# Eleven more edge-convolution steps projected in the largest-scores stage; early skip and mix fills moved into six written-out rounds of the scores pass

## The reference, cut to what matters

```python
e  = einsum('ehd,ehd->eh', q[src], k[dst]) * scale     # scores pass
m  = segment_max(e, dst)                               # largest-scores stage
ex = exp(e - m[dst])                                   # attention pass, with its sums per node
agg = segment_sum(ex / denom[dst] * v[src], dst)
skip = feat @ Wskip.T + bskip                          # "skip" fills; out*gate @ Wproj are the "mix" fills
msg = (edge_attr @ W_edge.T + b_edge) * h[src]         # edge convolution, 384 -> 256 per edge
agg = segment_sum(msg, dst)
fx = proj(expmap0(ft + b_res))                         # ball attention's last norm, taken up in the top stage
```

## Time and profile before

| what | value |
|---|---|
| median of 3 runs | 2938.04 us (2937.12 to 2939.76) |
| the profiled execution's own time | 2938.99 us |
| span of the profile (first to last instruction) | 2937.3 us |
| TensorE (PE) busy | 2614.2 us, 89% |
| VectorE (DVE) busy | 2130.9 us, 73% |
| ScalarE (ACT) busy | 1402.0 us, 48% |
| GpSimd (POOL) busy | 1069.7 us, 36% |

### The profile page before, as it was taken

The page is one execution under the profiler, slowest core; times in us unless marked ns, Lnnn a source line. Parts: engine busy times, 40 slices in busy tenths (PEclk is TensorE's granted clock), DMA queues, the critical chain, the costliest instruction groups (busy, mean ns, idle before and its releaser), DMA issues. The chain is left out here.

```text
span 2937.3 us, 54945 instructions
## 1 busy us (share of the span) xinstructions
PE 2614.2 (89%) x11923; PEld 2052.7 (70%) x11926; DVE 2130.9 (73%) x4283; ACT 1402.0 (48%) x2975; POOL 1069.7 (36%) x1184
## 2 busy tenths in 40 slices
PE   8777788779998999999989999999789978779698
PEld 6555555465556777777768888999678866657587
DVE  6687777868889665765348888888899969955321
ACT  3324323129884343443434444444489958755122
POOL 1677777722111000000016777666300018800043
PEclk9999999989999999999999999999889989989799
DMA  4799999937776100000036777667401130043343
GB/s 160 253 314 309 313 314 310 317 73 229 230 227 222 65 1 10 10 1 10 9 112 216 231 223 230 215 214 214 134 27 41 41 135 3 1 183 108 107 159 128
DMA packets 238294, 447.78 MB, mean 152 GB/s; under 512 B 29441, under 2 KB 127809, under 8 KB 236764
## 3 DMA queue, kind: packets, MB, share of 16 engines
q1 hardware_dynamic: 181214, 265.82, 27.7%
q0 software_dynamic: 56960, 180.47, 20.0%
HBM read 353.30 MB, written 93.87 MB: 152 GB/s over the span
## 5 line engine op out<-in xcount | busy, mean ns | idle before, releaser
L2065 PE MATMUL bank<-sums 128*128 128x256 f32 x2208 | 508.7, 381 | 2.0 <-PEq L117 1.6
L2164 POOL DMA_INDIRECT conv_h<-table_h,conv_ix x392 | 389.4, 993 | 241.0 <-ACT conv_ix L2125 152.8
L2065 PEld LDWEIGHTS bank<-sums 128*128 128x128 f32 x2208 | 408.6, 191 | 50.3 <-issue 2.0
L1840 ACT ACTIVATE area<-bank,nodes_bi,nodes_sc 128x320 f32<-128x320 f32 x320 | 197.4, 617 | 333.6 <-PE bank L1697 333.6
L731 POOL DMA_INDIRECT x<-table_qv,scores_ix x300 | 283.9, 946 | 162.2 <-ACT scores_ix L627 84.0
L2034 DVE SCALAR_TENSOR_TENSOR x<-bank,nodes_w,x 128x256 f32<-128x256 f32 x200 | 96.4, 483 | 215.7 <-PE bank L1708 215.6
L1454 PE MATMUL bank<-attend_pv,x 128*128 128x260 f32 x800 | 220.1, 404 | 26.7 <-POOL attend_pv L1384 24.6
L751 PE MATMUL bank<-sums,area 128*128 x800 | 224.2, 407 | 11.1 <-issue 5.9
L1454 PEld LDWEIGHTS bank<-attend_pv,x 128*128 128x128 f32 x800 | 137.5, 191 | 109.0 <-issue 62.5
L2125 ACT ACTIVATE conv_ix<-src 128x2 int32 x196 | 39.9, 203 | 336.1 <-DVE conv_msg L2188 329.3
L2204 DVE TENSOR_TENSOR sums<-sums,bank 64x256 f32 x392 | 163.8, 418 | 48.2 <-issue 36.3
(11 more groups left out here) (504 smaller groups left out, 5858.3 us busy)
## 6 DMA issues: line engine op xcount, KB each, us to landing
sums<-in_edges SPq DMA_DIRECT2D x184, 384.0 KB, 4.0
x<-edge_v SPq DMA_DIRECT2D x200, 256.0 KB, 3.0
edge_v<-x SPq DMA_DIRECT2D x150, 256.0 KB, 4.7
hidden_rows<-top_wide SPq DMA_DIRECT2D x25, 512.0 KB, 3.2
top_wd<-in_top_wd SPq DMA_DIRECT2D x8, 1024.0 KB, 13.7
projected<-spline_hst SPq DMA_DIRECT2D x8, 960.0 KB, 4.5
ball_hT<-projected SPq DMA_DIRECT2D x4, 1920.0 KB, 17.5
x<-in_x SPq DMA_DIRECT2D x10, 640.0 KB, 8.9
```

Of the source, the lines that this page charges most:

```text
L1840: nc.scalar.activation((h1, h2)[layer][:, o, hf * CW:(hf + 1) * CW], banks[n % HIDS][:, 0:CW], ACT.Relu, scale=sc[:, layer, e, o:o + 1], b ...
L2065: mm = nc.tensor.matmul(banks[u][:, g * F:(g + 1) * F], m.conv_eT[:, u, g, c], m.conv_w[:, c], start=False, stop=c == EC - 1, skip_group_c ...
L2164: nc.gpsimd.indirect_dma_start(out=h[:, u, g, :], out_offset=None, in_=m.d_h, in_offset=bass.IndirectOffsetOnAxis(ap=ix[:, u * G + g:u * G ...
```

## The change

- `AHEAD_STEPS` becomes 23 = `AHEAD_FIRST` 11 + `AHEAD_LAST` 12. The 12 stay in `node_layers`; the 11 are projected in `largest_scores`, 6 before the first scan's transposes and 5 before the second's, with edges loaded and results stored by SP. The loop in `edge_convolution` that takes one step of eight from `edges_ahead` then runs 23 passes.
- Of the early fills, 17 move into six written-out rounds (`FILLED` = 6) of the scores pass behind `MIXED`, two in the first and three in each of the others; 6 stay in the last round, 5 in the largest-scores stage.
- `FEWEST` becomes 2 * 23 + 3 = 49 for rounds of `UN` and `MIXED` + 6 + 2 = 30 for rounds of `RING` (26 and 24 before).
- SP loads the weights and bias for the 11 steps, 384 KB and 128 KB, in the scores pass.
- The start of the attention pass works in halves, with the clearing shared between ScalarE and GpSimd.
- At the end of the ball attention the first five tiles' roots, scaling and lengths are done, so that `lengths(0)` and `add(0)` leave the top stage.

```diff
+AHEAD_FIRST, AHEAD_LAST = 11, 12
+AHEAD_STEPS = AHEAD_FIRST + AHEAD_LAST
+FILLED = 6
+FEWEST = {UN: 2 * AHEAD_STEPS + 3, RING: MIXED + FILLED + 2}
-AHEAD_STEPS = 12
-FEWEST = {UN: 2 * AHEAD_STEPS + 2, RING: MIXED + 2}
...
-EARLY_IN_SCORES = 6
-EARLY_BESIDE_SCANS = (9, 8, 5)
+FILLS_AT = [{5: 0, 7: 1}] + [{1: 3 * k + 2, 4: 3 * k + 3, 7: 3 * k + 4} for k in range(FILLED - 1)]
+FILLS_IN_ROUNDS = sum(len(at) for at in FILLS_AT)
+EARLY_IN_SCORES = FILLS_IN_ROUNDS + 6
+EARLY_BESIDE_SCANS = (0, 0, len(EARLY_TILES) - EARLY_IN_SCORES)
+AHEAD_BESIDE_SCANS = (6, 5, 0)
...
@@ scores pass: SP, ScalarE, TensorE
                 sp.dma_start(m.wproj, a["mix_wproj"]).then_inc(early_loaded, 16)
+                sp.dma_start(m.ahead_w, a["gnn1_wedge"]).then_inc(ahead_loaded, 16)
+                sp.dma_start(m.ahead_b, a["gnn1_bedge"]).then_inc(ahead_loaded, 16)
+                sp.dma_start(m.first[:, 0:2 * UN * AHEAD_FIRST], m.d_steps[:, 0:2 * UN * AHEAD_FIRST]).then_inc(ahead_loaded, 16)
...
-                with act.Fori(MIXED + 1, rounds_of(act, m, RING)) as r:
+                for n, fills_at in enumerate(FILLS_AT):
+                    for u in range(RING):
+                        sources(MIXED + 1 + n, u)
+                        if u in fills_at:
+                            keep_early(fills_at[u])
+                with act.Fori(MIXED + 1 + FILLED, rounds_of(act, m, RING)) as r:
...
-                with pe.Fori(MIXED, last) as r:
+                for n, fills_at in enumerate(FILLS_AT):
+                    words = words_here()
+                    for u in range(RING):
+                        step(MIXED + n, u, words)
+                        if u in fills_at:
+                            early(fills_at[u])
+                    carry(words)
+                with pe.Fori(MIXED + FILLED, last) as r:
...
@@ largest-scores stage: SP, TensorE, ScalarE
+                for j in range(AHEAD_FIRST):
+                    edges_ahead(j)
+                    if j >= IN:
+                        store_ahead(j - IN)
...
+                def ahead(part):
+                    for j in steps_ahead(part):
+                        pe.wait_ge(ahead_in[j % IN], 16 * (j // IN + 1))
+                        pe.wait_ge(ahead_seeded, j + 1)
+                        for g in range(G):
+                            for k in range(EC):
+                                mm = nc.tensor.matmul(ahead_bank(j)[:, g * F:(g + 1) * F], ahead_eT[:, j % IN, g, k], m.ahead_w[:, k], start=False,
+                                                      stop=k == EC - 1, skip_group_check=True)
+                        mm.then_inc(ahead_made, 1)
...
-                early(0)
+                ahead(0)
...
-                    early(j + 1)
+                    ahead(j + 1)
+                pe.wait_ge(ahead_kept, AHEAD_FIRST)
+                early(2)
...
@@ attention pass: SP, start
-                sp.dma_start(m.first, m.d_steps[:, 0:2 * UN * AHEAD_STEPS]).then_inc(vec_loaded, 16)
+                sp.dma_start(m.first[:, 0:2 * UN * AHEAD_LAST], m.d_steps[:, 2 * UN * AHEAD_FIRST:2 * UN * AHEAD_STEPS]).then_inc(vec_loaded, 16)
+                sp.dma_start(m.first[:, 2 * UN * AHEAD_LAST:], m.d_steps[:, 0:UN]).then_inc(vec_loaded, 16)
...
@@ ball attention: ScalarE, VectorE
+                    if t == NT - 1:
+                        first_lengths(0, 2)
                     act.wait_ge(o_turned, t + 1)
...
+                first_add(0, 1)
                 keep(NT - 2)
+                first_add(1, U)
                 keep(NT - 1)
...
@@ top stage
-                lengths(0)
+                act.sem_inc(far_sq, U)
+                act.sem_inc(far, 1)
                 bend(0)
...
-                add(0)
-                add(1)
                 floor(0)
+                dve.sem_inc(added, U)
...
                 result(0)
                 normal(0)
+                add(1)
```

More of the change, by code:

```diff
@@ L119, in _ @@
         def _(sp):
[L120 to L124, removed]
+            clear_semaphores(nc, sp)
 def mean_and_variance(nc, c, stats, mv, work):
@@ L910, in _ @@
                         spread_out(last, u + UN - 1, words[-1])
[L911 to L917, removed]
+                    here = EARLY_IN_SCORES - FILLS_IN_ROUNDS
+                    for fill in range(u * here // RING, (u + 1) * here // RING):
+                        early(FILLS_IN_ROUNDS + fill)
             @block.vector
@@ L1103, in largest_scores, with steps_ahead, ahead_bank @@
         early_made, early_kept = st.sem("early_made"), st.sem("early_kept")
+        ahead_opened, ahead_seeded, ahead_made, ahead_kept = (
+            st.sem(x) for x in ("ahead_opened", "ahead_seeded", "ahead_made", "ahead_kept"))
+        IN, BANKS = 3, 3
+        ahead_eT = st.sb("ahead_eT", [P, IN, G, EC, P])
+        ahead_in = [st.sem(f"ahead_in{u}") for u in range(IN)]
+        ahead_stored = [st.sem(f"ahead_stored{u}") for u in range(2)]
+        def steps_ahead(part):
+            first = sum(AHEAD_BESIDE_SCANS[:part])
+            return range(first, first + AHEAD_BESIDE_SCANS[part])
+        def ahead_bank(j):
+            return banks[5 + j % BANKS][:, 0:G * F]
         def fills(part):
@@ L1367, in _ @@
                 distance(word, 0, 1)
+                for k, part in enumerate(halves):
+                    act.wait_ge(diff, 4 + k)
+                    nc.scalar.activation(m.probs[:, part], m.probs[:, part], ACT.Exp, scale=float(HD) ** -0.5).then_inc(exps, 1)
                 with act.Fori(0, last) as r:
@@ L1596, in _ @@
                     sp.dma_start(to, a[x]).then_inc(loaded, 16)
-                for j in range(IN_RING, AHEAD_STEPS):
+                for j in range(IN_RING, AHEAD_LAST):
                     edges_ahead(j)
@@ L1628, in _ @@
                         for u in range(OUT_RING + 2):
-                            sp.wait_ge(ahead_stored[u], 16 * sum(ahead_slot(j) == u for j in range(AHEAD_STEPS)))
+                            sp.wait_ge(ahead_stored[u], 16 * sum(ahead_slot(j) == u for j in range(AHEAD_LAST)))
                         sp.wait_ge(outs, TU * XQ * U)
@@ L1736, in _ @@
                 pe.wait_ge(ahead_w_in, 16)
-                for j in range(AHEAD_STEPS - 1):
+                for j in range(AHEAD_LAST - 1):
                     project_ahead(j)
@@ L2594, in output, with first_lengths @@
                     nc.scalar.activation(oT[:, t % 2], banks[6][:, 0:OC], ACT.Copy).then_inc(o_copied, 1)
+                def first_lengths(begin, end):
+                    for t in range(begin, end):
+                        act.wait_ge(first_added, t + 1)
+                        if t:
+                            act.wait_ge(first_squared, t)
+                        nc.scalar.activation(junk[:, 0:F], m.rows[:, t], ACT.Square, accum_out=far[:, t:t + 1]).then_inc(first_squared, 1)
                 for t in range(2):
```

161 lines of the change are left out of this document (120 added, 41 removed).

## The result

The changed kernel takes 3129.86 us (median of 4 runs, 3126.88 to 3131.05) where the kernel before takes 2937.58: ratio 1.0646, 95% interval 1.0633 to 1.0658, +192 us. The forecast was 3126 in a range of 3062 to 3150, and slower. The profiled execution takes 3131.05 us, with a span of 3129.1, 191.8 longer than before's.

A forecast was written before the change was run, and what follows sets the result against it. GpSimd's pace bounds the scores pass now, with DMA engines close behind; TensorE bounds attention and convolution. Terms 157.6 + 46.7 + 2 + 5 + 0.5 - 20.8 - 3 = +188.0 on 2938.99 give 3127.0, 3126 at the median; range 3062 to 3150.

The forecast's parts named there:

- The counts: Scores and attention passes: the least number 30 decides the rounds, so each grows from 200 to 240 steps, 40 of them padding.
- The padding steps: Scores pass: 40 added steps at 3.94 us, bound by DMA engines through slow gathers of one row, +157.6 us; chance 0.69.
- The rival of GpSimd's pace: Scores pass: padding steps keep 2.50 us each, 100 us in place of 157.6, total 3068 us; chance 0.20.
- The Trainium skill's rule that the prediction weighed: Scores pass: a padding step's DMA takes an estimated 1.8 us whatever its addresses, GpSimd's pace stays the bound, whole sum +130.
- The attention pass: Attention products: 40 added steps with the same TensorE work, 1.168 us each, +46.7 us.
- The fills: Scores pass: 17 fills moved into rounds, hidden except the first one's wait for weights; +2 us, ends 0 and 6.
- The largest-scores stage: Eleven projected steps there make the two scans' transposes 2.8 and 2.3 us late; +5 us, ends 0 and 19.
- The ring of three loads: Largest-scores stage: loads issued only when a slot is free could cost 14 us more in all.
- the faster start: Attention pass start: waiting for `edge_v`, it gains nothing from faster Exp and clearing; one more load, +0.5 us, ends 0 and 1.
- The convolution: Convolution messages: eleven more periods with one step of eight ready save 1.89 us each, -20.8 us, ends 0 and -30.
- The top stage: Ball attention to top stage: Tanh comes earlier as scaling and lengths leave, despite a later ScalarE copy; -3, ends 0 and -5.

The follow-up runs named there:

- the rounds alone: The kernel before with only its least number of rounds of eight raised from 24 to 30: 3146.25 us, ratio 1.0703.
- the kernel with spread rows: The changed kernel with its 688 padding entries naming 688 different rows of table_qv in place of row 0: 3065.71 us, ratio 1.0423.
- the two kernels with early skip weights: 25 rounds, five steps in the largest-scores stage, skip weights loaded behind round 17: 2929.6 us; the same with one fill moved and padding on 688 rows: 2928.93 us.

## Why the prediction was right, step by step

**The counts.** `FEWEST[RING]` = 30 became the number of rounds of both passes, as forecast; the rounds alone give +207.

**The padding steps.** 3.89 us against 3.94, and for the reason given: the gathers' queue at 5.92 us for a MB, DMA engines at 0.98. The rival of GpSimd's pace had 100 us, with the slow gathers an effect of the emptying queue; with full rounds they stayed slow, and they became fast with other rows in them. Its price was right for that case: 94 us were measured. The Trainium skill's rule that the prediction weighed, a fixed part and bytes over a rate whatever the addresses are (DMA: Bandwidth & Descriptors, section Anatomy of one DMA), leaves GpSimd's pace as the bound, and as soon as there are two rows that is what the runs show; by it the sum was +130, and the kernel with spread rows has +126 over its before. The page's rate itself is not seen: with spread rows the DMA engines, 0.96 busy, moved 315 GB/s, not 436. The same page's case of streams that meet in one part of HBM at half their rate (section Latency and other measured facts) agrees in size, 5.92 against 3.19; the row pitch that it speaks of was not tried.

**The attention pass.** 281.1 / 240 = 1.171 us a step against 1.168.

**The fills.** Hidden, but for the first one, whose price was mis-sized: rounds 22 to 24 took +4.3 in place of +2, within its bounds of 0 and 6. The prediction had the weights landing 5.9 us after an issue at 556.9; in the run the load was issued at 564.0, since the whole pass was 7 us late, and 7.3 us went by until the fill began. TensorE stood still 4.63 us, as forecast (some 4), but the fill then took 3.60 us in place of 1.89, which was not in the sum, and GpSimd stopped for 3.74 us, where about 1 had been left to it. Nor was it GpSimd's pace that hid the other fills of these rounds. Before, VectorE went through rounds 22 and 23 in 17.8 and 17.1 us, under GpSimd's 20.0, since it was behind and worked off GpSimd's lead; so VectorE's own work covered the fills (round 23 took 17.7 us with three of them), and its stop counted in full: round 22 took 24.5 us. Round 24 gave 2.9 us of that back, 17.6 in place of 20.5; before, it is the last round, with six fills and with the padding's slow gathers behind it (18.6 where those name 688 rows).

**The largest-scores stage.** +2.4 with the attention's start, in place of +5.5. The steps took 2.64 us (15.81 for six) and not 2.74, and the transposes came late by the right mechanism but less: VectorE waited 2.57 and 1.98 us for them, where 2.8 and 2.3 had been worked out and before had 0.9 in all.

```profile
778.61 15.81 PE L1198 MATMUL bank<-vec,largest_ahead_eT 128*128 128x256 f32 x72 [1.27 <-DMA largest_ahead_eT<-in_edges]
...
794.71 0.25 DVE L1283 COPY largest_scan_in<-bank 4x99 f32<-4x99 f32 x1 [2.57 <-PE bank L1216]
...
809.56 0.25 DVE L1283 COPY largest_scan_in<-bank 4x99 f32<-4x99 f32 x1 [1.98 <-PE bank L1216]
```

The ring of three loads cost nothing behind the first load. VectorE's first product of the attention pass waited 4.56 us for `edge_v`, so the faster start indeed gains little: 0.5 us.

**The convolution.** Eleven more periods, -21.5 in place of -20.8; 22 periods between the 23 messages take 494.9 us, 22.50 each:

```profile
L2290 DVE TENSOR_TENSOR conv_msg<-bank,conv_h x173: 691/691/693, 1752.3 to 2304.2; 128x512 f32<-128x512 f32 x173
L2290 DVE TENSOR_TENSOR conv_msg<-sums,conv_h x23: 683/686/697, 1773.9 to 2268.8; 128x512 f32<-128x512 f32 x23
```

**The top stage.** From the last message to Tanh -3.6, of which only 1.6 lies behind ScalarE's last pass over `ball_out` (2571.32 in the trace before, 2763.31 here), about half of the -3. ScalarE's timeline after, for the earlier trace rows:

```profile
2763.31 0.63 ACT L2694 ACTIVATE ball_junk<-ball_out 128x512 f32<-128x512 f32 x1 [3.11 <-DVE ball_out L2802]
...
2765.49 0.58 ACT L2700 ACTIVATE ball_oT<-bank 128x512 f32<-128x512 f32 x1
...
2770.59 1.28 ACT L3021 ACT_TABLE_LOAD   x1 [2.59 <-PEq L2641]
2771.89 0.21 ACT L3021 ACTIVATE xT<-xT 128x5 f32<-128x5 f32 x1
```

The copy for the last product stands behind two of the five lengths, as worked out. What the sum did not have is TensorE's clock. Its last product, before and after:

```profile
2572.69 2.00 PE L2718 MATMUL bank<-ball_wres,ball_oT 128*128 128x256 f32 x8 [0.69 <-ACT ball_oT L2594]
...
2766.11 3.60 PE L2848 MATMUL bank<-ball_wres,ball_oT 128*128 128x256 f32 x8 [2.12 <-ACT ball_oT L2700]
```

TensorE waited 2.12 us for the later copy and then ran the product at a granted clock of 0.54, where before it had 1.00: 1.6 us more. ScalarE has its lengths and roots by 2768.0 and waits 2.59 us for TensorE to end the ball attention. Where the slow product falls differs: in the two other profiles with before's code here (its rounds raised, and its padding on 688 rows) it is the product ahead, 3.2 us, and the stretch takes 11.6 us in place of 10.2; in the two kernels with early skip weights it is that one too, and the stretch takes 7.4 in place of 8.6. So the move was worth 1.6 us in this pair and 4.2 where the last product kept its pace. The other 2.0 of the -3.6 and the +1.4 behind Tanh are of the size by which the same code differs between executions: from the last message to the last pass over `ball_out` it took 457.2 to 461.1 us in the three profiles of before's code, and behind Tanh 354.9 to 357.2 in all profiles.

**What was in no term.** The +7.5 up to round 21 is not the change's: 5.4 of it is in rounds 5 to 9, whose code is the same in all these kernels, where this execution had a granted clock of 0.83 and before's 0.90. These five rounds took between 101.9 and 108.7 us in the profiled executions of all kernels here, and the last step of round 21 stood anywhere from 541.6 to 553.4. It hides the errors of the other sign: without it the sum would be +184 and the forecast 4 us too high. That the forecast meets this pair of executions so closely is in part luck; whether the other runs, whose medians are 192 us apart too, were late there as well, they don't show.

## What to carry to other kernels

A constant that names a least number of rounds is worth as much attention as the work that moves: compare it with the count of rounds that the trace shows, for every pass that uses it. Padding work is priced by its own addresses: here a padding step cost 3.89 us with all reads on one row and 2.3 to 2.4, GpSimd's pace, with two rows or more, so point padding at several rows, and do not add rounds of it. Work moved into a pass bound by another engine is hidden only if its operands are there when the engine arrives; load them when their place is free, and add to the price of a wait of TensorE that what follows may run at the lower clock. Balance what goes in their stead against the wait that ends last there.

## What the runs showed of the hardware

Gathers that all read one row of 2 KB took 5.9 us for a MB of the 16 DMA engines, and 3.1 to 3.3 with two, eight or 688 rows, also when each gather kept to one row. A stop of TensorE of 4.63 us was followed by a fill of 3.60 us in place of 1.89 at a granted clock of 0.54, the lower of its two levels (1.2 of 2.4 GHz) for most of it; a wait of 2.12 us in the ball attention was followed by a product of 3.60 us in place of 2.00, at 0.54 too. In padding rounds in which it was busy 100 of 156 us the granted clock was 0.74, and 0.96 where the same rounds took 94 us.
